# Layer norms inside the stages around them, in an eight-layer kernel on one core

## The reference

```python
def _layernorm(x, axis=-1, eps=1e-05):
    m = jnp.mean(x, axis=axis, keepdims=True)
    v = jnp.var(x, axis=axis, keepdims=True)
    return (x - m) / jnp.sqrt(v + eps)
```

```python
y = layernorm(x)                       # the layer's own norm
h = layernorm(y) * ln1_w + ln1_b       # the norm of its attention part
h = conv3(h)                           # causal, 3 taps, per channel
y = y + attention(h @ attn_w) @ proj_w # softmax, rope
h = layernorm(y) * ln2_w + ln2_b
x = x + y + experts(h)                 # 4 experts, routed by argmax(h @ router_w)
```

## Time and profile before

| | |
|---|---|
| median of 3 runs | 2646.72 us (2646.5 to 2649.6) |
| the profiled execution | 2643.61 us, its span 2641.8 us |
| granted PE clock, mean | 0.915 |
| PE busy | 81% |
| DVE busy | 69% |
| ACT busy | 52% |
| POOL busy | 14% |
| DMA, mean | 31 GB/s |

### The profile page before, as it was taken

The page is one execution under the profiler, slowest core; times in us unless marked ns, Lnnn a source line. Parts: engine busy times, 40 slices in busy tenths (PEclk is TensorE's granted clock), DMA queues, the critical chain, the costliest instruction groups (busy, mean ns, idle before and its releaser), DMA issues. The chain is left out here.

```text
span 2641.8 us, 39751 instructions
## 1 busy us (share of the span) xinstructions
PE 2139.3 (81%) x13146; PEld 943.1 (36%) x13324; DVE 1833.2 (69%) x4630; ACT 1376.9 (52%) x1968; POOL 362.9 (14%) x608
## 2 busy tenths in 40 slices
PE   3689999946799736557999998998347999999898
PEld 2123332224344424422233323665222233322565
DVE  6688788656577766668878874334968888884433
ACT  3246666772599643333566666222533566667221
POOL 4000110010454304100001001000000001101000
PEclk8699999987899868769999999999669999999899
DMA  7501020001011000061011000000052010000000
GB/s 193 140 1 37 2 38 1 1 1 48 31 51 45 18 0 1 0 189 36 1 38 38 1 1 1 1 0 0 0 163 61 1 38 21 18 1 1 1 0 16
DMA packets 48073, 81.68 MB, mean 31 GB/s; under 512 B 6348, under 2 KB 37836, under 8 KB 47228
## 3 DMA queue, kind: packets, MB, share of 16 engines
q1 hardware_dynamic: 42408, 71.34, 10.7%
q0 software_dynamic: 2528, 5.65, 0.7%
q10 hardware_dynamic: 2976, 2.67, 0.4%
HBM read 56.18 MB, written 23.07 MB: 30 GB/s over the span
## 5 line engine op out<-in xcount | busy, mean ns | idle before, releaser
L854 ACT ACTIVATE probs<-score 128x1024 f32<-128x1024 f32 x960 | 825.5, 896 | 522.8 <-PE score L918 519.7
L976 DVE TENSOR_REDUCE max_part<-stat 128x1 f32<-128x512 f32 x1152 | 722.0, 683 | 113.0 <-PE stat L868 110.4
L931 PE MATMUL pv<-probs,v_ones 128*9 128x512 f32 (+3 forms) x3840 | 443.7, 534 | 2.2 <-issue 1.0
L973 DVE CUSTOM_DVE_ANT_0 masked_scores<-stat,mask_row 128x128 f32<-128x128 f32 (+3 forms) x768 | 343.1, 487 | 102.2 <-PE stat L868 98.9
L868 PE MATMUL stat<-first_group_k,first_group_q 128*128 128x512 bf16 (+3 forms) x924 | 293.2, 371 | 91.1 <-DVE max_part L976 37.1
L828 POOL TENSOR_SCALAR_AFFINE_SELECT probs<-probs 128x256 f32<-128x256 f32 x384 | 154.0, 406 | 1249.3 <-ACT probs L854 1245.9
L868 PE MATMUL stat<-group_k,group_q 128*128 128x512 bf16 (+3 forms) x933 | 281.2, 348 | 18.3 <-DVE max_part L976 9.8
L918 PE MATMUL score<-first_group_q,first_group_k 128*128 128x512 bf16 (+3 forms) x921 | 253.3, 355 | 14.7 <-DMA first_group_q<-row_max_turned 8.3
L918 PE MATMUL score<-group_q,group_k 128*128 128x512 bf16 (+3 forms) x915 | 244.8, 348 | 10.1 <-DMA group_q<-row_max_turned 3.5
L1952 ACT ACTIVATE gate<-gate_ps 128x512 f32<-128x512 f32 x128 | 76.4, 597 | 262.0 <-PE gate_ps L1927 262.0
L868 PEld LDWEIGHTS stat<-first_group_k,first_group_q 128*128 128x128 bf16 x960 | 94.0, 99 | 269.3 <-DVE max_part L976 123.4
(11 more groups left out here) (308 smaller groups left out, 2353.9 us busy)
## 6 DMA issues: line engine op xcount, KB each, us to landing
q_parts<-parts_t SPq DMA_DIRECT2D x40, 384.0 KB, 4.0
group_k<-k_parts SPq DMA_DIRECT2D x18, 384.0 KB
group_q<-q_parts SPq DMA_DIRECT2D x18, 384.0 KB
k_parts<-parts_t SPq DMA_DIRECT2D x16, 384.0 KB, 4.9
head_q<-q_parts SPq DMA_DIRECT2D x48, 96.0 KB
head_k<-k_parts SPq DMA_DIRECT2D x48, 96.0 KB
first_group_k<-k_parts SPq DMA_DIRECT2D x9, 384.0 KB
first_group_q<-q_parts SPq DMA_DIRECT2D x9, 384.0 KB
```

The source lines that it names most:

```text
L854: nc.scalar.activation(probs[:, n % PSLOTS, :, 0:width], sc[hp][:, :, 0:width], ACT.Exp, scale=scale).then_inc(expd.sem, 1)
L931: last = nc.tensor.matmul(acc[32 * h:32 * h + D + 1, f:BANK], v9[:, kt, g * HG + h, :], probs[:, (2 * t + h // 2) % PSLOTS, h % 2, 0:BANK ...
L973: nc.vector.tensor_tensor_reduce(masked[:, at % 2, 0:width], ring[n % RBANKS][:, 0:width], w["mask_row"][:, BANK - width:BANK], 1.0, NEG, ...
L976: nc.vector.reduce_max(into, ring[n % RBANKS][:], AX.X).then_inc(stat_used.sem, 1)
```

## The change

The function `layer_norm` and `conv_stage` go. Class `RowStats` takes a block's statistics behind the sum that completes it, in the stage that writes X (or y). Class `Norm` holds the rest and is called inside the stage that reads: `norm.dve` (three tiles of each block), `norm.act` (the fourth tile and all four copies), `norm.turn` on PE, and `norm.wait` ahead of a block's first reader. Its banks are PSUM banks that the reading stage has anyway. `twice=True` computes both norms of the convolution layer from the statistics of x alone: if v is the variance of x, that of y is v / (v + eps), so the inverse deviation of both norms together is 1 / sqrt((v + eps) * eps + v). The first norm's rows, y, are then written by ACT (`first_norm`) later. `convolve` works by block. The first layer of the program takes its statistics in the reader (`known=False`). EARLY becomes 2.

```diff
-EARLY = 3
+EARLY = 2
...
+class RowStats:
+    def __init__(self, k, w, src):
+        self.nc, self.src, self.raw, self.mv = k.nc, src, w["row_stats"], w["row_mv"]
+        self.read, self.ready = k.counter("row_stats_read"), k.counter("row_stats_ready")
+    def take(self, q):
+        for i in range(QC * q, QC * q + QC):
+            ins = self.nc.vector.bn_stats(self.raw[:, i, :], self.src[:, i, :])
+        ins.then_inc(self.read.sem, 1)
+    def gather(self, dve, q):
+        dve.wait_ge(self.read.sem, self.read.at(q + 1))
+        for i in range(QC * q, QC * q + QC):
+            ins = self.nc.vector.bn_aggr(self.mv[:, i, :], self.raw[:, i, :])
+        ins.then_inc(self.ready.sem, 1)
+    def follow(self, dve, q, rows):
+        if q >= 1:
+            dve.wait_ge(rows.sem, rows.at(q))
+            self.take(q - 1)
+        if q >= 2:
+            self.gather(dve, q - 2)
+        if q == NQ - 1:
+            dve.wait_ge(rows.sem, rows.at(NQ))
+            self.take(NQ - 1)
+            self.gather(dve, NQ - 2)
+            self.gather(dve, NQ - 1)
...
+    def dve(self, dve, between=None, hook=None):
+        nc, mv, std, rstd = self.nc, self.mv, self.std, self.rstd
+        chain = Chain(dve, self.step)
+        if not self.known:
+            for i in range(NT):
+                ins = nc.vector.bn_stats(self.raw[:, i, :], self.src[:, i, :])
+            chain(ins)
+            for i in range(NT):
+                ins = nc.vector.bn_aggr(mv[:, i, :], self.raw[:, i, :])
+            chain(ins)
+        ins = nc.vector.tensor_scalar(std[:, 0], mv[:, :, 1], self.eps, None, ALU.add)
+        if self.twice:
+            chain(ins)
+            ins = nc.vector.scalar_tensor_tensor(std[:, 1], std[:, 0], self.eps, mv[:, :, 1], ALU.mult, ALU.add)
+        ins.then_inc(self.var_ready.sem, 1)
+        if between:
+            between()
+        dve.wait_ge(self.std_ready.sem, self.std_ready.at(1))
+        chain(nc.vector.reciprocal(rstd[:], std[:]))
+        nc.vector.scalar_tensor_tensor(self.shift[:], bcast(mv[:, :, 0], 1, self.N), -1.0, rstd[:], ALU.mult, ALU.mult).then_inc(self.scale_ready.sem, 1)
+        for n, q in enumerate(self.order):
+            for i in range(QC * q, QC * q + QC - 1):
+                ins = nc.vector.tensor_scalar(self.dst[:, i, :], self.src[:, i, :], mv[:, i, 0:1], rstd[:, self.N - 1, i:i + 1], ALU.subtract, ALU.mult)
+            ins.then_inc(self.dve_rows.sem, 1)
+            if hook:
+                hook(n)
...
+    def act(self, act):
+        nc = self.nc
+        act.wait_ge(self.var_ready.sem, self.var_ready.at(1))
+        nc.scalar.sqrt(self.std[:], self.std[:]).then_inc(self.std_ready.sem, 1)
+        act.wait_ge(self.scale_ready.sem, self.scale_ready.at(1))
+        def row(n):
+            self.act_tile(self.dst, self.N - 1, QC * self.order[n] + QC - 1).then_inc(self.act_rows.sem, 1)
+        row(0)
+        for n, q in enumerate(self.order):
+            if n + 1 < NQ:
+                row(n + 1)
+            act.wait_ge(self.turned.sem, self.turned.at(n + 1))
+            out = self.dst_t[:, q * BANK:(q + 1) * BANK]
+            if self.affine is None:
+                ins = nc.scalar.copy(out, self.banks[n])
+            else:
+                ins = nc.scalar.activation(out, self.banks[n], ACT.Identity, bias=self.affine[1][:, 0:1], scale=self.affine[0][:, 0:1])
+            ins.then_inc(self.kept.sem, 1)
+    def convolve(self, dve, q):
+        nc, at, cw = self.nc, q * BANK, self.w["conv_w"]
+        chain = Chain(dve, self.conv_step)
+        chain.n = 2 * q
+        here = self.conv[:, at:at + BANK]
+        dve.wait_ge(self.kept.sem, self.kept.at(q + 1))
+        chain(nc.vector.tensor_scalar(here, self.dst_t[:, at:at + BANK], cw[:, 2:3], None, ALU.mult))
+        for tap in (1, 0):
+            lag = 2 - tap
+            first = lag if q == 0 else 0
+            ins = nc.vector.scalar_tensor_tensor(self.conv[:, at + first:at + BANK], self.dst_t[:, at + first - lag:at + BANK - lag], cw[:, tap:tap + 1],
+                                                 self.conv[:, at + first:at + BANK], ALU.mult, ALU.add)
+            if tap == 1:
...
+    def turn(self, pe, n):
+        q = self.order[n]
+        pe.wait_ge(self.dve_rows.sem, self.dve_rows.at(n + 1))
+        pe.wait_ge(self.act_rows.sem, self.act_rows.at(n + 1))
+        for i in range(QC):
+            ins = self.nc.tensor.transpose(self.banks[n][:, i * P:(i + 1) * P], self.dst[:, QC * q + i, :], self.w["ident"][:])
+        ins.then_inc(self.turned.sem, 1)
...
@@ output_stage
-                for i in range(NT):
-                    dve.wait_ge(ready.sem, ready.at(i + 1))
-                    nc.vector.tensor_tensor(x[:, i, :], out[:, i % 4, 0:C], x[:, i, :], ALU.add).then_inc(used.sem, 1)
+                for q in range(NQ):
+                    dve.wait_ge(ready.sem, ready.at(q + 1))
+                    tiles = x[:, QC * q:QC * q + QC, :]
+                    nc.vector.tensor_tensor(tiles, out[:, q, :].rearrange("p (i c) -> p i c", c=C), tiles, ALU.add).then_inc(used.sem, 1)
+                    stats.follow(dve, q, used)
...
@@ project_stage: the tensor block
+                norm.turn(pe, 0)
                 for n, ((chunks, dst, bias), i) in enumerate(units):
+                    if n % (QC * len(jobs)) == 0:
+                        if i // QC + 1 < NQ:
+                            norm.turn(pe, i // QC + 1)
+                        norm.wait(pe, i // QC)
...
@@ qkv_stage: the tensor block
                 def project(c):
+                    norm.wait(pe, c)
...
+                norm.turn(pe, 0)
+                norm.turn(pe, 1)
                 project(0)
+                norm.turn(pe, 2)
+                norm.turn(pe, 3)
                 project(1)
...
@@ qkv_stage: the scalar block
+                norm.act(act)
                 if not biased:
                     evacuate(0)
...
                     nc.scalar.copy(turned_sb[:, n % 2, :, 1, :], rest[:, n % 2]).then_inc(second_cut.sem, 1)
+                    if norm.twice:
+                        norm.first_norm(first_norm, n)
                 if rows:
-                    load_rows(act, EARLY - 1)
+                    load_rows(act, 1)
...
@@ qkv_stage: the vector block
+                def conv_ahead(n):
+                    if norm.conv is not None and n >= 2:
+                        norm.convolve(dve, n - 2)
+                norm.dve(dve, hook=conv_ahead)
...
                 prepare(0, lambda: None)
                 for n in range(NQ):
+                    if norm.conv is not None and n + 2 < NQ:
+                        norm.convolve(dve, n + 2)
                     if n + 1 < NQ:
...
@@ qkv_stage: the sync block
-                    if rows and 0 < c < EARLY:
-                        load_rows(sp, c - 1)
+                    if rows and c == 1:
+                        load_rows(sp, 0)
...
@@ spline_ffn_stage
                 for c in range(2):
                     for half in range(2):
+                        norm.turn(pe, 2 * c + half)
+                    for half in range(2):
+                        norm.wait(pe, 2 * c + half)
...
+                    stats.follow(dve, q, out_used)
...
@@ rwkv_stage
+                norm.turn(pe, 0)
+                norm.turn(pe, 1)
...
                     for q in range(NQ):
+                        if n == 0:
+                            if q + 2 < NQ:
+                                norm.turn(pe, q + 2)
+                            norm.wait(pe, q)
...
                 nc.scalar.activation(wa[:, 0, :], w["wT"][:, 8, :], ACT.Copy, scale=w["mix"][:, 0:1]).then_inc(wa_ready.sem, 1)
+                norm.act(act)
                 nc.scalar.activation(wneg[:], w["decay"][:], ACT.Exp).then_inc(w_ready.sem, 1)
...
+                norm.dve(dve, between=mix_weights)
...
@@ experts_stage
+                norm.turn(pe, 0)
+                norm.turn(pe, 1)
                 for i in range(NT):
+                    if i % QC == 0:
+                        if i // QC + 2 < NQ:
+                            norm.turn(pe, i // QC + 2)
+                        norm.wait(pe, i // QC)
...
+                    if e < 0:
+                        block_stats(n)
+                def block_stats(n):
+                    tiles = [n * QC - QC + s for s in range(QC)]
+                    dve.wait_ge(out_used.sem, out_used.at(n * (E * QC)))
+                    for i in tiles:
+                        xi = x[:, bass.ds(i, 1), :].rearrange("p o c -> p (o c)")
+                        ins = nc.vector.bn_stats(w["row_stats"][:, bass.ds(i, 1), :].rearrange("p o s -> p (o s)"), xi)
+                    ins.then_inc(stats.read.sem, 1)
...
+                for q in range(NQ - 1):
+                    stats.gather(dve, q)
                 add_out(NQ, -1)
+                stats.gather(dve, NQ - 1)
```

262 lines of the change are left out of this document (118 added, 144 removed).

## The result

The changed kernel takes 2636.5 us as the median of six runs (2633.6 to 2639.9), the kernel before in the same comparison 2648.5; the ratio is 0.9953, 95% interval 0.9943 to 0.9964. That is 12 us less, where 41 were predicted: the direction was right, the size was not, and the time lies outside the range of 2594 to 2619.

What follows compares the result with a forecast made beforehand. No engine bounds the whole program; the change acts on seams between stages. Terms 3.4 + 2.6 + 0.8 + 2.7 + 7.4 + 0.7 - 0.5 + 19.2 + 6.0 - 1.3 = 41.0 us off the median 2646.72 gave 2605, range 2594 to 2619.

Steps and rivals of the forecast that it cites:

- Part 1: Seams between stages: statistics follow the writer's sums, DVE tail 3.16 us, square root 1.6 us sooner per spline seam.
- Part 2: Norm's block start: ACT's square-root table load loses its cover beside the statistics, 1.1 us lost in each of six seams.
- Rival (e): A table switch holds ACT once more for a load's length: 8 us more, 2613; 4%.
- Part 3: Reading stages: norm and turning move inside, reader starts after one turned block; retention 3.4 with statistics, linear 2.6, experts 3.7 twice.
- Router matmuls now run between the transposes ... 3.7, twice: Experts seams: routing chain ends R+11.15 against 14.7 to the first hidden product; 3.7 us gained in each of two.
- rival (a): PE's clock stays at 1.2 GHz through the shorter seams: gain only 30 to 33 us, 2615; 20%.
- Part 4: Convolution layers: second norm vanishes (8.9 us), convolution goes by block, rope at R+13.1; 9.6 us gained per layer, 19.2.
- Blocks 2 and 3 ... DVE the bound: 3.5 lost: Convolution layers: convolutions of blocks 2 and 3 queue on DVE ahead of preparing blocks 1 and 2; 3.5 us lost.
- Part 5: Attention starts: EARLY 3 to 2 lets SP store at once, stages start 2 to 3.7 us earlier; 6.0 gained, bounds 3 and 11.
- I take 2.0 in each of three: Three attention stages: from a start 2 to 3.7 us earlier, 2.0 us gained in each, 6.0 in all.
- rival d: Slower: attention stages wait for block 2's rows at unit 2, 17 us each giving 2655; 3%.
- rival (b): More is hidden: table loads 6.6, earlier attention starts 5, shorter ACT queue 3; gain 53, 2593; 14%.

Runs made afterwards that it cites:

- 1: EARLY put back from 2 to 3 in the changed kernel; 0.9937 of the kernel before, 4 us less than the changed kernel.
- run 3: Changed kernel with PE's second turning of q and k waiting for the four copies, not the four convolutions; 0.9935 of the kernel before.
- 5: Changed kernel with both EARLY 3 and PE's second turning waiting for the copies alone; 2628.6 us, 0.9921 of the kernel before.
- run 6: ACT evacuates block 0 ahead of copying blocks 2 and 3, against the changed kernel with EARLY 3 and the copies-only wait; 0.9908 of the kernel before.
- 9: Experts norm turned in one piece before router matmuls, against the changed kernel with EARLY 3 and the copies-only wait; 0.9932 of the kernel before.
- the last four runs: All-edits version less one edit each: identity turnings 0.9869, one-piece experts turning 0.9819, early table load 0.9878, statistics at the writer 0.9927.
- the three comparisons: EARLY 2 against EARLY 3 in the changed kernel, the all-edits version and the kernel before; EARLY 2 cost 4.2, 1.8 and -1.6 us.
- run 10: Changed kernel plus EARLY 3, copies-only wait, earlier ACT evacuation, identity turnings, early table load, one-piece experts turning, no last experts statistics; 2600.6 us, 0.9823.

## Why the prediction was right or wrong

- **Part 1, statistics at the writer: right.** Tail 3.02 us (3.16), 2.08 us less from the last sum to the square root; less is left after output stages, because the last add comes up to 1.1 us late. In the experts loop they cost 0.8 a stage (0.5 taken, bounds 0 to 3.3).
- **Part 2, the cover of the table load: right**, 1.05 us measured against 1.1. Rival (e) is out.
- **Part 3, reader after one block: half right.** Retention's reader at R + 2.70 (2.75), linear -2.3 (2.6), spline 2 -2.9 (2.7). Spline 1 lost 0.6: knots at R + 8.4 in this trace, but 9.4 to 9.9 in those of five kernels with the same order of norm and knots (1, 3, 5, 6, 9), not R + 8.1. rwkv's scan at R + 9.8 and not 9.25, its Exp behind the last copy as computed. **The step that failed** is "Router matmuls now run between the transposes ... 3.7, twice". I computed the seam as a chain of dependences at the clock of before (and hedged only 20% on the clock, with 4 us for both stages together). Of the 4.6 us in that term, 3.5 lie between R and the first hidden product (14.7 to 11.15); for the other 1.1 the text has no working. Measured, R comes 1.0 sooner after the last sum in both, but the first hidden product 0.9 and 0.7 later after R; with their output stages and loops the two lost 3.7 and 1.7: 12.8 us beside the forecast, the largest miss, 8.6 of it between R and the first hidden product. The mechanism is rival (a), and the last four runs show it: with the change's order of work the first hidden product comes at R + 15.6 at a clock of 0.50 and at R + 11.0, about the 11.15 computed, at 0.89. Its price was mis-sized: I thought of a clock that rises later, and it didn't rise before the first products. The output stages lost to it too: 3.4 us at 0.50 at the start of two of the three behind attention, some 1.2 us each.
- **Part 4, double norm: first half right** (R 11.1 us earlier than the second R was, 8.4 of it from the output stage on, 8.9 computed; rope at R + 13.0). **The step that failed** is "Blocks 2 and 3 ... DVE the bound: 3.5 lost": the time from the first rope operation to the last cut grew by 7.0. 1.3 us a layer by the trace, 2.4 by the ratios, was PE's wait for a convolution that it didn't need (run 3), a wait that the change added and that I didn't list. 4.1 are the convolutions in the queue. The rest is a path that the term leaves out: from the convolution over PE's projection, at a clock of 0.63, and ACT's evacuation to the second cut, 1.15 and 1.24 of waiting where it was 0.17 (run 3). ACT's order was called right (run 6: 5.0 us for all three layers).
- **Part 5, EARLY: wrong.** The stages start 1.7, 3.0 and 3.3 us sooner (2 to 3.7 forecast). **The step that failed** is "I take 2.0 in each of three", as if a stage that starts sooner ended sooner: the first score came 2.1, 0.3 and 1.2 us later after the last cut. I looked for what could eat this in the rows of block 2 (rival d, which didn't come: PE never waited for rows) and not in the small transfer queued behind them. A gain of 6 us was forecast; the three comparisons gave -4.2, -1.8 and +1.6. That the small transfer waits behind the large ones is read from the order of issue and the waits; no run moved it alone.
- **The sum:** by the runs, EARLY 4 to 10 and PE's wait about 5; by the traces, the experts about 13: 22 to 28 of the 29 us that the medians lack. Retention (2.1) and spline 1 (1.4) stand against a first layer that was 2.3 better; one execution can't settle these. Three sums don't hold as written: 3.1 less 1.1 ahead of rwkv is 2.0 and not 1.7 (1.6 measured), part 4 counts as a gain the 0.15 that part 2 calls a loss, and the items of rival (b) make a gain of 55.6 and not 53. None changes the account.

## What to carry to other kernels

When a pause of PE is shortened, cost the matmuls behind it at the low clock first, and look at what PE does in the pause: here neither a shorter pause nor work in it paid much alone, and both together paid more than their sum (2628.6 to 2600.6 with the smaller edits). Give every wait that an edit adds its line in the sum, with the question whether it names the event it needs. And ahead of making a transfer larger or earlier, list the small ones issued behind it.

## What was not expected of the hardware

- Edits that were worth 2.7 and 5.0 us alone were worth 12 and 15 beside the others (each good to 6 or 7 us), through PE's granted clock; its mean over the program went from 0.915 of full speed to 0.925.
- PE was busy without a gap from 1647.0 on in the first experts stage of the changed kernel, router matmuls first and products then, and still ran at 1.2 GHz until 1660.2.
- The same code in two executions of the same seam differs by 3.0 us with the clock (0.94 and 0.85), so that stage steps of two single profiles are good to 3 us, not to 0.3.
- In the second and third attention stage the first score came 2.9 to 4.1 us after the issue of the row maxima with one block's columns in the loads issued 3 to 7 us ahead of it (EARLY 3), and 6.4 to 9.7 with two (EARLY 2). In the first stage with EARLY 3 it was 3.1 in run 10, where the loads were issued 6.3 us ahead, and 4.9 to 15.0 in the others, where they were issued 1.1 to 2.5 us ahead; why it can be 15.0 no run here explains.
